# Two graph layers written out turn by turn, the stage ahead of attention normalised on ScalarE, and three stages' weights transferred one block earlier

## What is computed

```python
# layer 0, graph part; its input is layernorm(x)
h = layer_norm(x, gamma, beta)                  # a second norm, on the first one's result
agg = einsum('bij,bjh->bih', adj, h)
conv = agg @ W_rel + b_rel + h @ W_root
x = input + relu(conv)                          # the outer residual is added as well
# layer 0, feed-forward part: a recurrence over the 128 tokens (the "recurrence" below)
# layer 1, graph part
adj_norm = adj / (sum(adj, -1) + EPS)
h = relu(concat([x, einsum('bnm,bmf->bnf', adj_norm, x)]) @ weight + bias)
# layer 1, feed-forward part: a router on the mean over tokens, two of 8 experts for each batch row
# layer 2, graph part: attention with 8 heads; q, k, v are x @ Wq.T, x @ Wk.T, x @ Wv.T
```

## Time and profile before

| | us |
|---|---|
| median of 3 runs | 2054.09 (2053.57 to 2059.69) |
| the profiled execution's own time | 2054.29 |
| its span in the trace | 2052.6 |

### The profile page before, as it was taken

One profiled execution on the slowest core, in us unless ns is written; L12 is line 12 of the kernel. 1 busy time (PEld: TensorE's weight loads), 2 busy tenths in 40 slices (PEclk: granted clock), 3 DMA queues, 4 the chain that ended last, 5 costly groups with the idle time before them and its releaser, 6 DMA issues. The chain is left out here.

```text
span 2052.6 us, 43609 instructions
## 1 busy us (share of the span) xinstructions
PE 1712.4 (83%) x13074; PEld 1406.3 (69%) x13074; DVE 1180.6 (58%) x4462; ACT 878.1 (43%) x2731; POOL 810.5 (39%) x1312
## 2 busy tenths in 40 slices
PE   4666999997674996679999779989999978884995
PEld 3555777776564996568888656769999945553663
DVE  5663333336884675659999864423333357763542
ACT  2333444443333664246666423326666635440000
POOL 3441000002331664531111167755656534553665
PEclk9888999998887998569999859999999989995886
DMA  2110000001001442000000131112222252105331
...
DMA packets 138132, 96.85 MB, mean 47 GB/s; under 512 B 25551, under 2 KB 128754, under 8 KB 137925
## 3 DMA queue, kind: packets, MB, share of 16 engines
...
...
## 5 line engine op out<-in xcount | busy, mean ns | idle before, releaser
L1198 POOL DMA_INDIRECT scratch_made<-FEAT x136 | 153.3, 1127 | 123.1 <-DVE FEAT L1487 120.0
L1356 ACT ACTIVATE FEAT<-BANKS,EXP 128x128 f32<-128x128 f32 x544 | 155.0, 368 | 82.7 <-PE BANKS L1309 82.7
L195 PE MATMUL BANKS<-ident,WA 128*128 128x128 f32 x256 | 55.6, 356 | 142.7 <-DVE WA L189 142.1
L1051 ACT ACTIVATE EXP<-BANKS,NEGMAX 128x128 f32<-128x128 f32 x512 | 139.0, 382 | 59.6 <-DVE NEGMAX L1063 59.6
L412 PE MATMUL BANKS<-FEAT,ident 128*128 128x256 f32 x588 | 150.0, 383 | 0.0
L1309 PE MATMUL BANKS<-FEAT 128*128 128x128 f32 x1088 | 145.5, 277 | 0.0
L1318 PE MATMUL BANKS<-AUX,FEAT 128*128 x1088 | 144.4, 276 | 0.4 <-ACT FEAT L1356 0.4
L195 PEld LDWEIGHTS BANKS<-ident,WA 128*128 128x128 f32 x256 | 36.8, 180 | 155.4 <-DVE WA L189 136.3
L1190 POOL DMA_INDIRECT scratch_sent<-FEAT,POS x128 | 123.6, 966 | 38.9 <-issue 37.5
L488 POOL COPY WF<-AUX 128x512 f32 (+1 forms) x16 | 17.5, 1099 | 303.1 <-POOLq L101 303.1
L1309 PEld LDWEIGHTS BANKS<-FEAT 128*128 128x128 f32 x1088 | 133.9, 194 | 0.0
...
## 6 DMA issues: line engine op xcount, KB each, us to landing
EXP<-in_L_ffn_W SPq DMA_DIRECT2D x128, 128.0 KB, 2.1
...
scratch_sent<-FEAT,POS POOLq DMA_INDIRECT x192, 2.3
```

Of the source, the lines that this page charges most:

```text
L195: last = pe.transpose(tile(ps, k), tile(src, k), ident[:])
L1051: last = act.activation(tile(EXS[:, par], 4 * k + n), tile(PS[j], c), ACT.Exp, bias=NEGMAX[:, par, 4 * k + n:4 * k + n + 1])
L1198: pool.indirect_dma_start(out=made2, out_offset=bass.IndirectOffsetOnAxis(ap=XI_I[:, t % R_IN, H:ROW2], axis=0), in_=YO[:, t % R_OUT, :], ...
L1356: last = act.activation(tile(HR[:, t % R_H], c), tile(PS[2 + t % 2], c), ACT.Gelu, bias=BT[:, c, t:t + 1])
```

## The change

In words, stage by stage:

- **Layer 0's graph stage** is unrolled. The in-place part `plain` makes `x * (r + 1) - m * r`, which is `x` plus its normalised value, in four instructions, in place of four into `WC` and an addition. `norm2` moves from DVE to ACT, which takes the scale and a negated mean times scale as its bias. POOL's chain for the twice normalised value has one `pow` on eight numbers in place of two in a row, and `dev2` gains two small instructions. Lags rise by one for the parts behind `hT`. The weights are issued from ACT's queue and `x` ahead of the adjacency.
- **The recurrence** also loads layer 1's graph weights. In each of its first 64 steps one of the filler matmuls is replaced by one that multiplies a stored adjacency tile by a column of ones: the row sums.
- **Layer 1's graph stage** loads no adjacency and neither sums, scales nor transposes it: the transposed tiles `AT` of layer 0 are the stationary or moving operands directly, and the sum's inverse is applied to the result. PE transposes the states straight from their strided place (64 floats from one token to the next), without POOL's copy. The result is token-major, so `back` is gone; both normalisations go to ACT. The router's and the experts' weights are issued in this block.
- **The experts' stage** also issues the attention's weights on SP: four behind the first four batch rows, and eight more, one for each of the next eight.
- **The stage ahead of the attention** has no load, no `WB`; normalisation is on ACT, the bias on DVE, and PSUM banks alternate.

The core of the diff:

```diff
...
-                    sp.dma_start(STAGE[:, par].rearrange("p (b j) -> p b j", b=G), dgroup(adj_v, i)).then_inc(sin, 16)
-                    sp.dma_start(cols(X, i).rearrange("p (b j) -> p b j", b=G), dgroup(x_v, i)).then_inc(sin, 16)
-                pipelined(sp, NG, [(0, load)])
+                    sp.dma_start(cols(X, i).rearrange("p (b j) -> p b j", b=G), x_v[i]).then_inc(sin, 16)
+                    sp.dma_start(STAGE[:, par].rearrange("p (b j) -> p b j", b=G), adj_v[i]).then_inc(sin, 16)
+                unrolled(NG, [(0, load)])
...
-                    normalise(v, i, par, WA, MV, RS, 4, s.xn)
-                    normalise(v, i, par, WC, MV, RS, 1, s.t4)
-                    v.wait_ge(s.t4, i + 1)
-                    v.tensor_tensor(cols(X, i), cols(X, i), WC[:, par], ALU.add).then_inc(s.x1, 1)
+                    for k in range(G):
+                        last = v.tensor_scalar(tile(WA[:, par], k), cols(X, i, GW, k * H, H), MV[:, par, k, 0:1],
+                                               PWB[:, par, 1, 1, k:k + 1], ALU.subtract, ALU.mult)
+                    last.then_inc(s.xn, 1)
+                def plain(i, par, half):
+                    for k in range(G):
+                        x = cols(X, i, GW, k * H, H)
+                        last = v.tensor_scalar(x, x, RS[:, par, 0, k:k + 1], RS[:, par, 1, k:k + 1], ALU.mult, ALU.subtract)
+                    last.then_inc(s.x1, 1)
...
-                def norm2(i, par, half):
-                    v.wait_ge(s.rstd2, i + 1)
-                    reused(v, s.x_ps, i, 2)
-                    normalise(v, i, par, WE, MVB, RSB, 1, s.xn2)
-                pipelined(v, NG, [(3, norm2), (1, norm), (0, stats), (2, add)])
+                unrolled(NG, [(0, stats), (1, norm), (3, add), (1, plain)])
...
+                    pool.wait_ge(s.mv, i + 1)
+                    pool.tensor_scalar(PWB[:, par, 0, 0, :], MV[:, par, :, 1], EPS, None, ALU.add).then_inc(s.var, 1)
+                    pool.tensor_scalar(PWB[:, par, 0, 1, :], MV[:, par, :, 1], 1.0 + EPS, EPS * EPS, ALU.mult, ALU.add).then_inc(s.var, 1)
+                    pool.wait_ge(s.var, 2 * i + 2)
+                    pool.tensor_tensor(PWB[:, par, 1], PWB[:, par, 0], mhalf[:].unsqueeze(1).to_broadcast([P, 2, G]), ALU.pow
...
+                    pool.tensor_tensor(RS[:, par, 1, :], MV[:, par, :, 0], PWB[:, par, 1, 0, :], ALU.mult)
+                    pool.tensor_scalar(RS[:, par, 0, :], PWB[:, par, 1, 0, :], 1.0, None, ALU.add).then_inc(s.r2, 1)
...
+                    pool.tensor_scalar(NEG[:, par], MVB[:, par, :, 0], -1.0, None, ALU.mult).then_inc(s.n2, 1)
                     inverse_deviation(pool, i, par, MVB, RSB, s.mv2, s.var2, s.rstd2)
...
+                unrolled(NG, [(0, dev), (3, dev2)])
...
+                def norm2(i, par, half):
+                    act.wait_ge(s.m2, i + 1)
+                    reused(act, s.x_ps, i, 2)
+                    for k in range(G):
+                        last = act.activation(tile(WE[:, par], k), cols(X, i, GW, k * H, H), ACT.Identity,
+                                              scale=RSB[:, par, 1, k:k + 1], bias=NMR[:, par, k:k + 1])
+                    last.then_inc(s.xn2, 1)
...
+                unrolled(NG, [(3, relu), (2, hT), (4, norm2), (2, hw), (0, adjT), (4, xT)])
...
-                pipelined(pe, NG, [(2, conv), (1, hT), (0, adjacency), (2, back), (1, project), (3, xT)])
...
+                unrolled(NG, [(2, hT), (3, back), (2, project), (0, adjacency), (4, xT), (2, conv)])
...
+                sp.dma_start(wtop, a["L1_gnn_weight"][0:H, :]).then_inc(s.w1, 16)
+                sp.dma_start(wbot, a["L1_gnn_weight"][H:2 * H, :]).then_inc(s.w1, 16)
+                sp.dma_start(b1rows, a["L1_gnn_bias"].partition_broadcast(P)).then_inc(s.w1, 16)
+                sp.wait_ge(s.w1, 3 * 16)
...
-                        for _ in range(2 if prefetch and u < 6 else 3):
+                        if step < B:
+                            pe.matmul(ROWSUM[:, step:step + 1], AT[:, step * T:(step + 1) * T], ones[:, 0:1], start=True, stop=True)
+                        for _ in range((2 if prefetch and u < 6 else 3) - (step < B)):
                             pe.matmul(PS[7][:, 0:half], ident[:], cols(FEAT, j, STEPS * B, 0, half), start=True, stop=True)
...
-                def load(i, par, half):
-                    reused(sp, s.adjT_ps, i, 2)
-                    sp.dma_start(STAGE[:, par].rearrange("p (b j) -> p b j", b=G),
-                                 dgroup(adj_v, i)).then_inc((s.in0, s.in1)[par], 16)
-                pipelined(sp, NG, [(0, load)])
...
+                sp.dma_start(wr1[:], a["L1_ffn_Wr"]).then_inc(load_r1, 16)
...
+                sp.dma_start(W2_1, a["L1_ffn_W2"].rearrange("e (c p) d -> p (e c) d", p=P)).then_inc(load_e1, 16)
...
-                def hidden(i, par, half):
-                    reused(pool, s.h_ps, i, 2)
-                    src = HS_v[:, G * i:G * i + G, :] if isinstance(i, int) else HS_v[:, bass.ds(i * G, G), :]
-                    pool.tensor_copy(WF[:, par].rearrange("p (b t) -> p b t", b=G), src).then_inc(s.h, 1)
...
+                unrolled(NG, [(4, dev2), (1, dev)])
...
-                    v.reduce_sum(ROWS[:, par, 0, :], STAGE[:, par].rearrange("p (b j) -> p b j", b=G), AX.X).then_inc(s.sum, 1)
...
+                def mix(i, par, half):
+                    v.wait_ge(s.agg, i + 1)
+                    v.wait_ge(s.root, i + 1)
+                    for k in range(G):
+                        last = v.scalar_tensor_tensor(tile(WD[:, par], k), tile(PS[4], k), INV1[:, 1, G * i + k:G * i + k + 1],
+                                                      tile(WF[:, par], k), ALU.mult, ALU.add)
+                    last.then_inc(s.mix, 1)
+                def add2(i, par, half):
+                    reused(v, s.m2, i, 2)
+                    v.wait_ge(s.mix, i + 1)
+                    v.scalar_tensor_tensor(cols(X, i), WD[:, par], 0.0, cols(X, i), ALU.max, ALU.add).then_inc(s.x2, 1)
+                    wait_apart(v, s.x2, i + 1)
+                    statistics(v, i, par, STATSB, MVB, s.raw2, s.mv2)
...
                 def add(i, par, half):
                     v.wait_ge(s.h_ps, i + 1)
+                    reused(v, s.m1, i, 2)
                     v.tensor_tensor(cols(X, i), cols(X, i), PS[0], ALU.add).then_inc(s.x1, 1)
...
+                unrolled(NG, [(4, mix), (4, add2), (1, add), (3, root)])
...
-                pipelined(v, NG, [(4, norm2), (2, norm), (1, add), (3, add2), (1, rows)])
...
+                unrolled(NG, [(3, xT), (2, norm), (5, norm2), (3, xw), (5, feat)])
...
                 def hidden(i, par, half):
-                    pe.wait_ge(s.h, i + 1)
                     reused(pe, s.x1, i, 1)
-                    transpose4(pe, PS[0], WF[:, par], s.h_ps)
-                def adjT(i, par, half):
-                    pe.wait_ge(s.adjn, i + 1)
-                    reused(pe, s.adjT, i, 1)
-                    transpose4(pe, PS[1], STAGE[:, par], s.adjT_ps)
+                    for k in range(G):
+                        last = pe.transpose(tile(PS[0], k), HS_v[:, G * i + k, :], ident[:])
+                    last.then_inc(s.h_ps, 1)
...
-                pipelined(pe, NG, [(3, conv), (2, xT), (0, hidden), (3, back), (2, adjT), (2, project), (4, feat)])
...
+                def aggregate(i, par, half):
+                    pe.wait_ge(s.xw, i + 1)
+                    reused(pe, s.mix, i, 1)
+                    for k in range(G):
+                        last = pe.matmul(tile(PS[4], k), cols(AT, i, GW, k * T, T), tile(WC[:, par], k), start=True, stop=True)
+                    last.then_inc(s.agg, 1)
+                unrolled(NG, [(3, xT), (0, hidden), (3, project), (3, root), (5, feat), (3, aggregate)])
...
-                in_turn(B, [(0, load)])
+                in_turn(R_W1, [(0, load)])
+                sp.wait_ge(s.pad, 1)
+                heads = lambda v: v.rearrange("i (h d) -> i h d", h=HEADS)
+                sp.dma_start(WqP[:, :, 0:HD], heads(a["L2_gnn_Wq_T"])).then_inc(load_a2, 16)
+                sp.dma_start(WkP[:, :, 0:HD], heads(a["L2_gnn_Wk_T"])).then_inc(load_a2, 16)
+                sp.dma_start(WvT, a["L2_gnn_Wv_T"]).then_inc(load_a2, 16)
+                sp.dma_start(bo_b, a["L2_gnn_bo"].partition_broadcast(P)).then_inc(load_a2, 16)
+                for i in range(R_W1, B):
+                    load(i)
+                    k = i - R_W1
+                    if k < HC * NC:
+                        tile_at, chunk = k // NC, k % NC
+                        h = HC * (tile_at % 2) + 2 * chunk + tile_at // 2
+                        at = HP * tile_at + HD * chunk
+                        sp.dma_start(WoP[at:at + HD, :], a["L2_gnn_Wo_T"][h * HD:(h + 1) * HD, :]).then_inc(load_a2, 16)
...
-                def keep(i, par, half):
-                    pool.wait_ge(s.xT, i + 1)
-                    pool.tensor_copy(cols(FEAT, i), WB[:, par]).then_inc(s.keep, 1)
```

(30 more changed lines are left out.)

322 lines of the change are left out of this document (154 added, 168 removed).

## The result

The changed kernel took 1941.87 us in its profiled execution (span 1940.1), 112 us less than before. The ratio of its times to those of before is 0.9445, 95% interval 0.941 to 0.9479. Its median is 1976.59 us because two of its four executions lay at 2011 and 2021 us; the ratio leaves them out, and the runs that change the recurrence's filler bear on them.

What follows compares the result with a forecast made beforehand. Chains of waits were taken to bound the three rewritten stages, PE the recurrence, with the clock behind them. Savings of 69 + 6 + 2.7 - 3 + 29 = 103.7 us from 2054.3 gave 1950 us, range 1918 to 1980.

Steps and rivals of the forecast that it cites:

- DVE's turn: Layer 0's graph stage: two statistics pairs, two groups of four and an addition, 5.34 us, taken as 5.5 with waits.
- the loop of PE and ACT: Layer 0's graph stage: the next bound behind DVE's work, summing to 5.1 us a turn at full clock.
- The term that the text gave to both, order and work together: Layer 0's graph stage: turns of 5.5 us for 10.0, the stage ending at 109 us, 69 us saved.
- The wait for POOL: Layer 0 before the change: DVE waited 28.7 us for POOL in 120 us, read as 2.4 of a 10.0 us turn.
- the forecast of 0: Recurrence: PE's work hides the added loads and row sums, so its 303 us change by 0.
- rival E: Recurrence: its clock falls to half, +1.4 us a step, 90 us over 64 steps, total 2040; chance 0.03, 0.02 beyond.
- The serial loop: Layer 1's graph stage: DVE's 3.7 us then PE's 4.0 set the turn, 7.8 us at full clock, 10.8 at half.
- the saving at the start: Layer 1's graph stage: weights already there save as much as the added lag turn costs, some 3 us.
- The term for the strided transposes: Layer 1's graph stage: PE's transposes of states read with a 256-byte step cost +0.4 us a turn.
- Router and experts' stage: Router: 2.7 us saved on waiting for weights; experts' stage: 3 us lost to added issues on SP's queue.
- rival B: Stage ahead of the attention gets the full clock, saving 18 us more, total 1932; chance 0.22.
- Rival C: Layer 0's graph stage keeps its slow clock and PE bounds it, total 1964 or 1996; chance 0.10.

Runs made afterwards that it cites:

- the one with one filler less: The changed kernel with one more 256-column filler matmul taken out in each of the recurrence's first 64 steps; ratio 0.9581 to the kernel before.
- the small filler: The changed kernel with one 128-column filler matmul added back in each of the recurrence's first 64 steps; ratio 0.947 to the kernel before.
- the ten traces without the filler: The filler is matmuls nobody reads, added to the changed kernel ahead of the attention (ratio 0.9448, stage 53.3 us); without it the stage took 53.3 to 62.0 us.

## Why the prediction was right

**Layer 0: right, and within 1 us partly by luck.** DVE's turn was worked out as 5.34 and taken as 5.5; it is 5.35, and DVE waits for 0.9 us in 13 turns. Fifteen turns are then 80 us and not 82.5, and what is left of the stage, its start and its last turns, is 29.7 us and not 26.5: the two made up for each other. ACT's group with a scale and a bias for each row was priced like DVE's, 1.11, and takes 1.64. The other terms of the loop of PE and ACT came out up to 0.1 us shorter each, and the loop, put at 5.1 us, measures 5.39 from one relu to the next (45.73 to 51.12). So the two stand level, and neither is cover for the other: put back on DVE at the best place tried, the group costs 13 to 14 us, as DVE's list has no slack. The term that the text gave to both, order and work together, divides into 35 and 33, the clock being part of both. The wait for POOL was read too low: the 28.7 us stand ahead of the 10 groups that the line counts (x40), 2.9 us a turn and not 2.4. The forecast made no use of it.

**The recurrence: the forecast of 0 held in the profile, but rival E was nearer than 0.03.** Its step as written was that PE's work hides the exchange, as "PE is busy in all of it". The busy time fell from 290 to 277 us, and the runs showed that what is at stake is the clock. With the same instructions the recurrence took 304 us or 377; at half clock it added 73 us, E's 64 steps of 1.15 and not of 1.4. Of 34 executions with the cut filler (all kernels of this study that have it, less the one with one filler less) 13 lay some 70 us above the others, and none of 16 with the small filler did. Four of the 13 are all the executions of one kernel, the one with layer 0's second normalisation early on DVE. No trace shows such an execution of the changed kernel itself; that it is the recurrence there too is inferred from the size, and from the filler's effect. Two of the changed kernel's four executions lay there, 61 and 71 us above the forecast. That 1950 came out for the profiled one is luck as far as this term goes.

**Layer 1: the loop right, the gain too small by 7 us and in the wrong place.** The serial loop, 7.8 us in the forecast, measured 8.02 at full clock, and behind the first two turns a turn takes 9.23 us on the mean, where 9.2 was forecast. But before the change these turns took 9.40 and not 9.6, so all 13 together gave only 2.3 of the 12.8 us. The other 10.4 came at the start, from DVE's first additions:

```profile
485.08 0.69 DVE L515 TENSOR_TENSOR X<-X,BANKS 128x512 f32<-128x512 f32 x1 [4.74 <-PE BANKS L195]
...
490.87 0.67 DVE L515 TENSOR_TENSOR X<-X,BANKS 128x512 f32<-128x512 f32 x1
```

Before the change the first one started 4.0 us into the stage, behind POOL's copy and a wait of 3.71 us of PE for the weights, and the first two turns took 5.8 us each, with the sums and the scaling in them. In the changed kernel:

```profile
414.57 0.69 DVE L553 TENSOR_TENSOR X<-X,BANKS 128x512 f32<-128x512 f32 x1
```

This is 1.0 us into the stage. The next addition starts at 416.65, and the first two turns take 2.1 us each, as no group has reached the mixing yet and the sums and the scaling are gone. The forecast put the saving at the start at some 3 us and set it against the added turn of lag; behind the last addition both kernels take the same (23.8 and 23.7 us). So the mis-sized term is the start: some 3 us, measured 10.4.

Three readings on the way were off and small beside it. The term for the strided transposes, +0.4 a turn, was 0.14 to 0.24. Its upper bound by the rows was 1.12 in place of 0.44, which is +0.7 and not +1.1. And a clock of 0.84 is full for 0.68 of the time, not of the turns, which gives 8.6 us a turn out of 7.8 and 10.8, not 8.8.
By the Trainium skill (page SBUF — State Buffer, section Door 1: The DMA port swizzle) each access that goes to another line of 16 bytes pays; here four loads took 0.66 against 0.42 us, which agrees in direction and is small beside a turn of 8.02.

**Router and experts' stage:** 2.5 for 2.7, and +2.3 for +3. The second came out nearly as forecast, and 1.4 of it is the wait for matrices that the forecast named, though for the ninth row's in this profile and not for the fifth's.

**Ahead of the attention: right in sum, one bound missed.** The turn at half clock was 3.6 as worked out: the group that starts at 771.66 is followed by the one at 775.26.

```profile
771.66 1.65 ACT L931 ACTIVATE WA<-X,NMR,RS 128x128 f32<-128x128 f32 x4
...
775.26 1.65 ACT L931 ACTIVATE WA<-X,NMR,RS 128x128 f32<-128x128 f32 x4
...
778.14 1.65 ACT L931 ACTIVATE WA<-X,NMR,RS 128x128 f32<-128x128 f32 x4
...
780.54 0.58 ACT L937 COPY FEAT<-BANKS 128x512 f32<-128x512 f32 x1 [0.28 <-PE BANKS L195]
```

At full clock it is 2.88 (775.26 to 778.14), not 2.4. The loop that the forecast left out runs from ACT's copy (777.66) to its four activations (778.14, 1.65 us), to PE's transposes of them (779.85, 0.66), to the next copy (780.54). ACT still waits 0.28 us for PE in each turn, so its work of 1.65 + 2 x 0.59 doesn't fill the turn; its order does. So rival B, which was to save 18 us, can save 9 at most (62.0 to 53.2), and part of that came by itself in eight of the ten traces without the filler.

**Rival C** didn't come: layer 0 ran at 0.97, with as many transposes among PE's work as before.
The rule that speaks for C, that transposes don't count as busy for the clock in the same way (the Trainium skill, TensorE: Matmul & The Clock Gate, Part 4: PE-mode transpose), didn't decide here: the share of transposes was four groups of seven and the clock was full. The profile shows them as MATMUL rows and doesn't say whether they run in the mode that the page means.
